# An LSTM recurrence on one core: ScalarE's gates and cell tanh go to PSUM, and the two O sigmoids become one

## The chip, the core and the metric

The kernel runs on one core of a Trainium2 chip. Its time is the device time of one execution in microseconds. Five engines work on it: TensorE (PE; its weight loads are the profile's PEld), VectorE (DVE), ScalarE (ACT), GpSimd (POOL), and SyncE (SP), which issues DMAs. They have queues of their own and meet only at semaphores. There are two on-chip memories: SBUF, and PSUM, in which matmuls leave their results, in 8 banks.

## The reference

The input `x` has 2 sequences of 1024 steps with 256 features. First a modulated projection is added to it, and then the outputs of an LSTM with 256 hidden values, whose start state is `cond_1024`:

```python
x = x + _L0_cond_ref(x, cond_1024, L0_cond_weight)
x = x + _L1_cond_ref(x, cond_1024, L1_cond_Wx, L1_cond_Wh, L1_cond_b)
...
xW = jnp.einsum('ntd,dk->tnk', x, Wx) + b
def step(carry, xw_t):
    prev_h, prev_c = carry
    a = xw_t + prev_h @ Wh
    i = jax.nn.sigmoid(a[:, :Hdim])
    f = jax.nn.sigmoid(a[:, Hdim:2 * Hdim])
    o = jax.nn.sigmoid(a[:, 2 * Hdim:3 * Hdim])
    g = jnp.tanh(a[:, 3 * Hdim:])
    next_c = f * prev_c + i * g
    next_h = o * jnp.tanh(next_c)
```

The 1024 steps depend on each other: `h` of one step is an operand of the next one's product with `Wh`.

## The kernel before, in words

**Before the loop** (about the first 90 us) the kernel transposes `x` so that features lie on the partitions, computes the projection and `xW` with large matmuls, and prepares `Wh` as two 16-bit parts, `wh_p`.

**The layout of a step.** The 256 hidden values are two chunks of 128 partitions (K = 2), and there are B = 2 sequences, so that a gate of a step has only CB = 4 columns. `h` too is kept in two 16-bit parts, `h_parts`; each gate chunk is the sum of products of both parts. All the operations on VectorE and ScalarE have 2 to 12 elements in each partition.

**The matmuls of a step** (`iteration` in the tensor block, L430 to L464; all are recorded at L302, the helper `mm`). First come 12 input matmuls, which put this step's `xW` into PSUM through an identity matrix (`ring`, `ident_b`): for the gates F, G and I seven of them, which wait for `c_done` (the new cell of the step before), and for O the last five, which wait for `o_act` (the sigmoids of O of the step before). Then come 44 matmuls with `h_parts`: 8 for the high part of I (wait `h_hi`), 8 for F (wait `h_lo`, signal `f_mm`), 8 for G (`g_mm`), 8 for the low part of I (`ig_in`), 4 for the first chunk of O (`o0_mm`), 8 for the second chunk of O (`o_mm`).

**The cell** is computed by VectorE and ScalarE in turns:

- L608 DVE sums the two parts of F; L692 ACT takes its sigmoid to `sig_f`; L612 DVE multiplies it by the old cell, into `scan_b`.
- L610 DVE sums G; L695 ACT takes the sigmoid of I and G together (G is computed as 2 sigmoid(2a) - 1, its weights being doubled), into `scan_in`.
- L614 DVE sums the first chunk of O; L697 and L699 ACT take the sigmoids of O's two chunks, into `scan_h`.
- L617 DVE, a scan over 12 elements (4 columns of 3), computes the new cell, reading two SBUF operands and writing PSUM (`c_done`); L701 ACT takes its tanh, into `scan_h` (`t_done`).
- L620 DVE multiplies sigmoid(O) and tanh into the high part of `h` (`h_hi`); L623, another scan, computes the low part (`h_lo`); L627 keeps `h` for the output.

GpSimd prepares the ring of inputs and adds `h` to `xt` in groups of four steps.

**The output** leaves in 8 blocks of 128 steps. In the first iteration of each later block, at four of its eight steps, PE transposes a 128 x 128 tile of the block before into `turned` (L464), and ScalarE copies it out (L707, signal `y_read`). Such a transpose happens 7 x 4 = 28 times. `turned` lies in the bank of G's sum, G_SUM; the transpose waits for `cell_in`, which says that ScalarE has read that bank, and PE waits for the copy (L452) behind the F products of the next step, ahead of its G products.

**What sets the order.** The order is the written order of each engine's block; there is no planner. The loops are L466 to L471: the first block of steps, and for each later block its iteration with transposes and then an inner loop without.

Of the kernel before, what the change touches and what calls it, by code (L numbers as in the profile page):

```python
# [27 lines left out]
P = 128  # L28
# [11 lines left out]
I_BANK, G_SUM, F_BANK, O_BANK, G_BANK, FO_SUM, CELL, O_REST = range(8)  # L40
# [3 lines left out]
def cond_resid_lstm(nc, x, cond, w, wx, wh, bias, out):  # L44
# [11 lines left out]
    with ExitStack() as ctx:  # L56
# [3 lines left out]
        def sem(name):  # L60
            return ctx.enter_context(nc.semaphore(name))
# [40 lines left out]
        scan_in = sb("scan_in", [P, 6 * CB + 2 + 2])  # L102
        scan_a = scan_in[:, 0:3 * CB].rearrange("p (c s) -> p c s", s=3)
        scan_b = scan_in[:, 3 * CB + 2:6 * CB + 2].rearrange("p (c s) -> p c s", s=3)
        sig_ig = scan_in[:, 2:6 * CB + 2].rearrange("p (h c s) -> p h c s", h=2, s=3)[:, :, :, 0]
# [10 lines left out]
        pre_f = banks[FO_SUM][:, 0:CB]  # L116
        pre_o = banks[FO_SUM][:, CB:CB + B]
        pre_g = banks[G_SUM][:, 0:CB]
        pre_ig = psum[:, I_BANK:G_SUM + 1, 0:CB]
        turned = banks[G_SUM][:, BANK - P:BANK]  # L120
# [25 lines left out]
        f_act, o0_act, o_act = sem("f_act"), sem("o0_act"), sem("o_act")  # L146
        cell_in, c_done, t_done = sem("cell_in"), sem("c_done"), sem("t_done")
# [146 lines left out]
        def _(pe):  # L294
# [135 lines left out]
            def iteration(i, n=None):  # L430

                t = i * UNROLL
                for u in range(UNROLL):
                    part = u - TILE_STEP
                    if u % HALF == 0:
                        pe.wait_ge(ring_full, 2 * i + u // HALF + 1)
                    pe.wait_ge(c_done, t + u + 1)
                    input_apart(GATE_F, u, 0, K)
                    input_apart(GATE_G, u, 0, K)
                    input_together(GATE_I, I_BANK, u, 0, K)  # L440
                    pe.wait_ge(o_act, t + u + 1)
                    input_apart(GATE_O, u, 0, 1)
                    last = input_together(GATE_O, O_REST, u, 1, K)
                    if u % HALF == HALF - 1:
                        last.then_inc(ring_used, 1)
                    pe.wait_ge(h_hi, t + u + 1)
                    products(GATE_I, I_BANK, 0, 0, K)
                    pe.wait_ge(h_lo, t + u + 1)
                    products_apart(GATE_F, 0, K).then_inc(f_mm, 1)
                    if n is not None and 0 < part <= B * K:  # L450

                        pe.wait_ge(y_read, n * (B * K) + (part - B * K))  # L452
                    products_apart(GATE_G, 0, K).then_inc(g_mm, 1)
                    products(GATE_I, I_BANK, 1, 0, K).then_inc(ig_in, 1)
                    products_apart(GATE_O, 0, 1).then_inc(o0_mm, 1)
                    products(GATE_O, O_REST, 0, 1, K)
                    products(GATE_O, O_REST, 1, 1, K).then_inc(o_mm, 1)
                    if n is not None and 0 <= part < B * K:

                        b, k = divmod(part, K)  # L460
                        if part == 0:
                            pe.wait_ge(y_whole, n)
                        pe.wait_ge(cell_in, (t + u + 1) * 2)
                        nc.tensor.transpose(turned, y_tile[:, k * B + b, :], ident[:, :]).then_inc(y_turned, 1)  # L464
# [16 lines left out]
        def _(dve):  # L481
# [80 lines left out]
            link(nc.vector.memset(scan_in[:, :], 0.0))  # L562
            nc.vector.memset(scan_a[:, :, 1], 2.0)
            nc.vector.memset(scan_b[:, :, 1], -1.0)
# [20 lines left out]
            nc.vector.memset(pre_f, 0.0).then_inc(h_lo, 1)  # L585
            nc.vector.memset(cell, 0.0).then_inc(c_done, 1)
# [15 lines left out]
            with dve.Fori(0, T // UNROLL) as i:  # L602
                t = i * UNROLL
                for u in range(UNROLL):
# [7 lines left out]
                    nc.vector.tensor_tensor(scan_b[:, :, 2], sig_f[:, :], cell[:, :, 2], ALU.mult).then_inc(cell_in, 1)  # L612
                    dve.wait_ge(o0_mm, step)
                    nc.vector.tensor_reduce(by_chunk(pre_o), parts_of(GATE_O, 1), AX.X, ALU.add).then_inc(o0_sum, 1)  # L614

                    dve.wait_ge(cell_in, both)
                    nc.vector.tensor_tensor_scan(flat(cell), flat(scan_a), flat(scan_b),  # L617
# [3 lines left out]
                                                   in1=scan_h[:, :, 2], op0=ALU.mult, op1=ALU.mult).then_inc(h_hi, 1)  # L621
                    dve.wait_ge(h_hi, step)
                    nc.vector.tensor_tensor_scan(flat(h_parts[:, 1, :, :]), flat(scan_h[:, :, :]), flat(h_parts[:, 0, :, :]),  # L623
# [12 lines left out]
        def _(act):  # L636
# [43 lines left out]
            act.sem_inc(t_done, 1)  # L680

            act.sem_inc(s_out, 16)

            def iteration(i, n=None):

                t = i * UNROLL
                for u in range(UNROLL):
# [59 lines left out]
```

## Times and profile before

| | |
|---|---|
| time, median of 3 runs | 2111.53 us (2111.23 to 2111.78) |
| span of the profiled execution, first to last instruction | 2109.4 us |
| median less span | 2.1 us |
| PE busy | 1884.8 us, 89% |
| PEld busy | 1744.9 us, 83% |
| DVE busy | 1250.0 us, 59% |
| ACT busy | 707.7 us, 34% |
| POOL busy | 480.7 us, 23% |

The span is what the profiled execution's own time was between its first and last instruction; the times of the runs contain 2.1 us more. Busy shares count an instruction from its start to its end; instructions of one engine overlap, and in a serial chain an engine with a low share can still be on the path. A timeline row has the start in us, the duration in us, the engine, the line, the operation and its tiles, and in brackets how long the engine was idle before it and who released it.

### The profile page before, as it was taken

How to read it: one execution, taken by the hardware profiler on the slowest of the kernel's cores; microseconds unless marked ns; L12 is line 12 of the kernel's file. 1: busy time of each engine (PE TensorE's matmuls, PEld its weight loads, DVE VectorE, ACT ScalarE, POOL GpSimd, SP SyncE). 2: the span in 40 equal slices, each digit the busy share in tenths (PEclk: the TensorE clock that was granted, in tenths of full speed). 3: DMA queues.
4: the chain of work that ended last, by engine and by line, in shares of the span. 5: the costliest groups of instructions: out<-in, count | busy, mean ns of one | idle time of the engine just before them, and what ended most of it. 6: DMA issues, size and time to landing. Idle time of an engine off the chain costs nothing. (4 is left out here: it accounts for less than half of the span.)

```text
span 2109.4 us, 138886 instructions
## 1 busy us (share of the span) xinstructions
PE 1884.8 (89%) x57612; PEld 1744.9 (83%) x57612; DVE 1250.0 (59%) x8257; ACT 707.7 (34%) x5179; POOL 480.7 (23%) x1298
## 2 busy tenths in 40 slices
PE   8999999999989998899989999899998999989998
PEld 5588888888878888888878888788887888878887
DVE  3366666666656665566656666566665666656665
ACT  2233333333333333333333333333333333333333
POOL 1122222222222222222222222222222222222221
PEclk9855555555555555555555555555555555555555
DMA  2000000000000000000000000000000000000000
GB/s 85 2 0 0 0 0 7 0 0 0 0 8 0 0 0 1 7 0 0 0 1 7 0 0 0 7 1 0 0 0 8 0 0 0 0 8 0 0 0 5
DMA packets 5214, 7.67 MB, mean 4 GB/s; under 512 B 268, under 2 KB 4632, under 8 KB 5144
## 3 DMA queue, kind: packets, MB, share of 16 engines
q1 hardware_dynamic: 4872, 6.30, 0.9%
q8 instruction: 66, 1.08, 0.2%
q10 hardware_dynamic: 272, 0.26, 0.0%
q14 instruction: 4, 0.03, 0.0%
HBM read 4.46 MB, written 2.10 MB: 3 GB/s over the span
## 5 line engine op out<-in xcount | busy, mean ns | idle before, releaser
L302 PE MATMUL psum<-h_parts,wh_p 128*128 128x2 f16 (+1 forms) x45056 | 1370.9, 166 | 12.6 <-issue 12.4
L302 PEld LDWEIGHTS psum<-h_parts,wh_p 128*128 128x128 f16 x45056 | 1286.7, 104 | 28.9 <-issue 12.8
L302 PE MATMUL psum<-ring,ident_b 128*128 128x4 bf16 (+2 forms) x12288 | 492.6, 168 | 202.1 <-DVE psum L617 179.2
L302 PEld LDWEIGHTS psum<-ring,ident_b 128*128 128x128 bf16 x12288 | 409.7, 105 | 286.2 <-DVE psum L617 260.3
L692 ACT ACTIVATE sig_f<-psum 128x4 f32<-128x4 f32 x1024 | 178.0, 174 | 1136.3 <-DVE psum L608 1136.3
L234 POOL CAST ring<-xw 128x64 bf16 (+1 forms) x256 | 121.3, 474 | 1447.2 <-POOLq L272 1413.2
L608 DVE TENSOR_REDUCE psum<-psum 128x4 f32<-128x8 f32 x1024 | 179.2, 175 | 430.9 <-PE psum L302 430.9
L620 DVE SCALAR_TENSOR_TENSOR h_parts<-scan_h 128x4 f16<-128x4 f32 x1024 | 176.5, 172 | 248.4 <-ACT scan_h L701 248.4
L697 ACT ACTIVATE scan_h<-psum 128x2 f32<-128x2 f32 x1024 | 178.2, 174 | 134.3
L610 DVE TENSOR_REDUCE psum<-psum 128x4 f32<-128x8 f32 x1024 | 179.1, 175 | 52.4 <-PE psum L302 13.5
L623 DVE TENSOR_TENSOR_SCAN h_parts<-scan_h,h_parts 128x12 f16<-128x12 f32 x1024 | 187.5, 183 | 35.1
L695 ACT ACTIVATE scan_in<-psum 128x8 f32<-128x8 f32 x1024 | 185.9, 182 | 56.9 <-PE psum L302 13.7
L617 DVE TENSOR_TENSOR_SCAN psum<-scan_in 128x12 f32<-128x12 f32 x1024 | 198.6, 194 | 0.1
L612 DVE TENSOR_TENSOR scan_in<-sig_f,psum 128x4 f32<-128x4 f32 x1024 | 166.0, 162 | 27.2
L701 ACT ACTIVATE scan_h<-psum 128x4 f32<-128x4 f32 x1024 | 181.0, 177 | 0.1
L614 DVE TENSOR_REDUCE psum<-psum 128x2 f32<-128x4 f32 x1024 | 175.1, 171 | 0.5
L699 ACT ACTIVATE scan_h<-psum 128x2 f32<-128x2 f32 x1024 | 172.0, 168 | 0.0
L627 DVE TENSOR_TENSOR hring<-scan_h 128x4 f32<-128x4 f32 x1024 | 154.6, 151 | 0.0
L240 POOL TENSOR_TENSOR ring<-rest,ring 128x64 bf16<-128x64 f32 x256 | 125.2, 489 | 47.6 <-POOLq L228 47.6
L238 POOL CAST ring<-rest 128x64 bf16<-128x64 f32 x256 | 120.7, 471 | 42.9 <-POOLq L228 42.9
L236 POOL TENSOR_TENSOR rest<-xw,ring 128x64 f32<-128x64 bf16 (+1 forms) x256 | 89.4, 349 | 46.3 <-POOLq L228 46.3
L245 POOL TENSOR_TENSOR xt<-xt,hring 128x16 f32 (+1 forms) x256 | 58.3, 228 | 14.8 <-DVE hring L627 14.8
(81 smaller groups left out, 221.8 us busy)
## 6 DMA issues: line engine op xcount, KB each, us to landing
x_rows<-in_x_dram SPq DMA_DIRECT2D x4, 512.0 KB, 8.6
out_dram<-y_rows SPq DMA_DIRECT2D x7, 256.0 KB, 2.1
wh_sb<-in_L_cond_Wh_dram SPq DMA_DIRECT2D x1, 1024.0 KB, 6.0
wx_sb<-in_L_cond_Wx_dram SPq DMA_DIRECT2D x1, 1024.0 KB, 10.9
w_sb<-in_L_cond_weight_dram ACTq DMA_DIRECT2D x1, 256.0 KB, 2.8
out_dram<-y_rows SPq DMA_DIRECT2D x2, 128.0 KB, 1.7
small_rows<-in_cond_dram SPq DMA_DIRECT2D x1, 2.0 KB
small_rows<-in_L_cond_b_dram SPq DMA_DIRECT2D x1, 4.0 KB
```

Of the source, the lines that this page charges most:

```text
L302: return nc.tensor.matmul(out_, lhs, rhs, start=first, stop=last, skip_group_check=True)
L608: nc.vector.tensor_reduce(by_chunk(pre_f), parts_of(GATE_F, K), AX.X, ALU.add).then_inc(f_sum, 1)
L610: nc.vector.tensor_reduce(by_chunk(pre_g), parts_of(GATE_G, K), AX.X, ALU.add).then_inc(ig_in, 1)
L614: nc.vector.tensor_reduce(by_chunk(pre_o), parts_of(GATE_O, 1), AX.X, ALU.add).then_inc(o0_sum, 1)
L617: nc.vector.tensor_tensor_scan(flat(cell), flat(scan_a), flat(scan_b), 0.0, ALU.mult, ALU.add).then_inc(c_done, 1)
L620: nc.vector.scalar_tensor_tensor(out=h_parts[:, 0, :, 2], in0=scan_h[:, :, 1], scalar=2.0 ** H_SCALE, in1=scan_h[:, :, 2], op0=ALU.mult, o ...
L623: nc.vector.tensor_tensor_scan(flat(h_parts[:, 1, :, :]), flat(scan_h[:, :, :]), flat(h_parts[:, 0, :, :]), 0.0, ALU.mult, ALU.subtract).t ...
L692: nc.scalar.activation(sig_f[:, :], pre_f, ACT.Sigmoid, scale=unscale).then_inc(f_act, 1)
L695: nc.scalar.activation(sig_ig, pre_ig, ACT.Sigmoid, scale=unscale).then_inc(cell_in, 1)
L697: nc.scalar.activation(scan_h[:, 0:B, 1], pre_o, ACT.Sigmoid, scale=unscale).then_inc(o0_act, 1)
L699: nc.scalar.activation(scan_h[:, B:CB, 1], banks[O_REST][:, B:CB], ACT.Sigmoid, scale=unscale).then_inc(o_act, 1)
L701: nc.scalar.activation(scan_h[:, :, 2], cell[:, :, 2], ACT.Tanh).then_inc(t_done, 1)
```

## The change

Four things are edited.

1. The sigmoids of I and G no longer go to SBUF (`scan_in`) but to PSUM (`gates`, in the bank G_SUM), and the cell scan reads them there. `scan_in` is now one operand of 12 elements in SBUF, with f times the old cell and the constants; the other operand is `gates`.
2. The tanh of the cell is computed twice: first to PSUM (`tanh_c`, signal `t_done`), where the product for the high part of `h` reads it, and then to SBUF (`scan_h`, signal `t_kept`), for the scan of the low part, which now waits for `t_kept` as well, and for the row of outputs.
3. The two sigmoids of O become one, which waits for `o0_sum` and `o_mm` and reads two neighbouring banks; for that the banks are put in another order, and the second chunk of O lies at the start of its bank.
4. `turned` moves from the bank G_SUM to O_BANK, in which the parts of O's first chunk are. The transpose now waits for `o0_sum`, VectorE's read of that bank, and not for `cell_in`; and PE's wait for `y_read` moves from ahead of the G products to ahead of the O input matmuls, since these write O_BANK.

```diff
-I_BANK, G_SUM, F_BANK, O_BANK, G_BANK, FO_SUM, CELL, O_REST = range(8)
+G_SUM, I_BANK, F_BANK, O_BANK, G_BANK, CELL, FO_SUM, O_REST = range(8)
...
-        scan_in = sb("scan_in", [P, 6 * CB + 2 + 2])
-        scan_a = scan_in[:, 0:3 * CB].rearrange("p (c s) -> p c s", s=3)
-        scan_b = scan_in[:, 3 * CB + 2:6 * CB + 2].rearrange("p (c s) -> p c s", s=3)
-        sig_ig = scan_in[:, 2:6 * CB + 2].rearrange("p (h c s) -> p h c s", h=2, s=3)[:, :, :, 0]
+        scan_in = sb("scan_in", [P, CB, 3])
...
+        pre_o0 = banks[FO_SUM][:, 0:B]
+        pre_o = psum[:, FO_SUM:O_REST + 1, 0:B]
         pre_g = banks[G_SUM][:, 0:CB]
-        pre_ig = psum[:, I_BANK:G_SUM + 1, 0:CB]
-        turned = banks[G_SUM][:, BANK - P:BANK]
+        pre_ig = psum[:, G_SUM:I_BANK + 1, 0:CB]
+        turned = banks[O_BANK][:, BANK - P:BANK]
+        gates = banks[G_SUM][:, 2 * CB:5 * CB].rearrange("p (c s) -> p c s", s=3)
+        sig_ig = gates[:, :, 1:3].rearrange("p c h -> p h c")
+        tanh_c = banks[G_SUM][:, 6 * CB:7 * CB]
...
                     pe.wait_ge(o_act, t + u + 1)
+                    if n is not None and 0 < part <= B * K:
+                        pe.wait_ge(y_read, n * (B * K) + (part - B * K))
                     input_apart(GATE_O, u, 0, 1)
...
                     products_apart(GATE_F, 0, K).then_inc(f_mm, 1)
-                    if n is not None and 0 < part <= B * K:
-                        pe.wait_ge(y_read, n * (B * K) + (part - B * K))
                     products_apart(GATE_G, 0, K).then_inc(g_mm, 1)
...
-                        pe.wait_ge(cell_in, (t + u + 1) * 2)
+                        pe.wait_ge(o0_sum, t + u + 2)
                         nc.tensor.transpose(turned, y_tile[:, k * B + b, :], ident[:, :]).then_inc(y_turned, 1)
...
-                    nc.vector.tensor_tensor(scan_b[:, :, 2], sig_f[:, :], cell[:, :, 2], ALU.mult).then_inc(cell_in, 1)
+                    nc.vector.tensor_tensor(scan_in[:, :, 2], sig_f[:, :], cell[:, :, 2], ALU.mult).then_inc(cell_in, 1)
...
-                    nc.vector.tensor_tensor_scan(flat(cell), flat(scan_a), flat(scan_b),
+                    nc.vector.tensor_tensor_scan(flat(cell), flat(gates), flat(scan_in[:, :, :]),
                                                  0.0, ALU.mult, ALU.add).then_inc(c_done, 1)
                     dve.wait_ge(t_done, step)
                     nc.vector.scalar_tensor_tensor(out=h_parts[:, 0, :, 2], in0=scan_h[:, :, 1], scalar=2.0 ** H_SCALE,
-                                                   in1=scan_h[:, :, 2], op0=ALU.mult, op1=ALU.mult).then_inc(h_hi, 1)
+                                                   in1=tanh_c, op0=ALU.mult, op1=ALU.mult).then_inc(h_hi, 1)
                     dve.wait_ge(h_hi, step)
+                    dve.wait_ge(t_kept, step)
...
                     act.wait_ge(o0_sum, step)
-                    nc.scalar.activation(scan_h[:, 0:B, 1], pre_o, ACT.Sigmoid, scale=unscale).then_inc(o0_act, 1)
                     act.wait_ge(o_mm, step)
-                    nc.scalar.activation(scan_h[:, B:CB, 1], banks[O_REST][:, B:CB], ACT.Sigmoid, scale=unscale).then_inc(o_act, 1)
+                    nc.scalar.activation(scan_h[:, :, 1].rearrange("p (h b) -> p h b", b=B), pre_o, ACT.Sigmoid, scale=unscale).then_inc(o_act, 1)
                     act.wait_ge(c_done, step)
-                    nc.scalar.activation(scan_h[:, :, 2], cell[:, :, 2], ACT.Tanh).then_inc(t_done, 1)
+                    nc.scalar.activation(tanh_c, cell[:, :, 2], ACT.Tanh).then_inc(t_done, 1)
+                    nc.scalar.activation(scan_h[:, :, 2], cell[:, :, 2], ACT.Tanh).then_inc(t_kept, 1)
```

ScalarE's queue of one step, before (the tiles are output<-input, then the output's shape):

```order
L692 ACTIVATE sig_f<-psum 128x4 [waits f_sum]
L694 REGISTER_ALU
L695 ACTIVATE scan_in<-psum 128x8 [waits ig_in]
L697 ACTIVATE scan_h<-psum 128x2 [waits o0_sum]
L699 ACTIVATE scan_h<-psum 128x2 [waits o_mm]
L701 ACTIVATE scan_h<-psum 128x4 [waits c_done]
```

ScalarE's queue of one step, after:

```order
L698 ACTIVATE sig_f<-psum 128x4 [waits f_sum]
L700 REGISTER_ALU
L701 ACTIVATE psum<-psum 128x2x4 [waits ig_in]
L704 ACTIVATE scan_h<-psum 128x4 [waits o_mm,o0_sum]
L706 ACTIVATE psum<-psum 128x4 [waits c_done]
L707 ACTIVATE scan_h<-psum 128x4
```

There are five activations in a step as before: one sigmoid of O less, one tanh more. The I/G sigmoid and the first tanh write PSUM.

PE's queue in the step behind a transpose, from the last input matmuls of I (`ring`) to the G products (`h_parts`), before:

```order
L302 MATMUL psum<-ring,ident_b 128x4 x3
L302 MATMUL psum<-ring,ident_b 128x4 [waits o_act]
L302 MATMUL psum<-ring,ident_b 128x2 x4
L302 MATMUL psum<-h_parts,wh_p 128x2 [waits h_hi]
L302 MATMUL psum<-h_parts,wh_p 128x2 x7
L302 MATMUL psum<-h_parts,wh_p 128x4 [waits h_lo]
L302 MATMUL psum<-h_parts,wh_p 128x4 x7
L452 ISA
L302 MATMUL psum<-h_parts,wh_p 128x4 [waits y_read]
```

The same piece of PE's queue, after:

```order
L305 MATMUL psum<-ring,ident_b 128x4 x3
L448 ISA [waits o_act]
L305 MATMUL psum<-ring,ident_b 128x4 [waits y_read]
L305 MATMUL psum<-ring,ident_b 128x2 x4
L305 MATMUL psum<-h_parts,wh_p 128x2 [waits h_hi]
L305 MATMUL psum<-h_parts,wh_p 128x2 x7
L305 MATMUL psum<-h_parts,wh_p 128x4 [waits h_lo]
L305 MATMUL psum<-h_parts,wh_p 128x4 x15
```

The wait for ScalarE's copy of the transposed tile stood behind 16 `h_parts` matmuls of the next step; now it stands ahead of all 44 of them and of the five input matmuls of O.

## Rows read from the trace of the kernel before

**Rows 1.** Head of the profile's page.

```profile
span 2109.4 us, 138886 instructions
```

**Rows 2.** Waits of the whole run: engine, line, releaser, us in total, times, longest.

```profile
DVE h_parts L620 <- ACT scan_h L701: 248.4, 1024, 0.2
```

**Rows 3.** Timeline of one ordinary step: start us, duration us, engine, line, operation.

```profile
1002.01 1.34 PE L302 MATMUL psum<-h_parts,wh_p 128*128 128x2 f16 x44
...
1002.64 0.17 DVE L608 TENSOR_REDUCE psum<-psum 128x4 f32<-128x8 f32 x1 [0.38 <-PE psum L302]
...
1002.85 0.17 DVE L610 TENSOR_REDUCE psum<-psum 128x4 f32<-128x8 f32 x1
...
1003.06 0.18 ACT L695 ACTIVATE scan_in<-psum 128x8 f32<-128x8 f32 x1
1003.17 0.17 DVE L614 TENSOR_REDUCE psum<-psum 128x2 f32<-128x4 f32 x1
1003.28 0.19 DVE L617 TENSOR_TENSOR_SCAN psum<-scan_in 128x12 f32<-128x12 f32 x1
1003.38 0.17 ACT L697 ACTIVATE scan_h<-psum 128x2 f32<-128x2 f32 x1
1003.45 0.17 ACT L699 ACTIVATE scan_h<-psum 128x2 f32<-128x2 f32 x1
1003.50 0.18 ACT L701 ACTIVATE scan_h<-psum 128x4 f32<-128x4 f32 x1
...
1003.53 0.48 PE L302 MATMUL psum<-ring,ident_b 128*128 128x8 bf16 x12 [0.18 <-DVE psum L617]
1003.71 0.17 DVE L620 SCALAR_TENSOR_TENSOR h_parts<-scan_h 128x4 f16<-128x4 f32 x1 [0.24 <-ACT scan_h L701]
1003.92 0.18 DVE L623 TENSOR_TENSOR_SCAN h_parts<-scan_h,h_parts 128x12 f16<-128x12 f32 x1
...
1003.94 1.34 PE L302 MATMUL psum<-h_parts,wh_p 128*128 128x2 f16 x44
```

**Rows 4.** Setup, by shape: count, busy us, mean ns; ScalarE reading SBUF.

```profile
L658 ACT ACTIVATE root<-var 128x4 f32<-128x4 f32 x1 | 0.2, 205 | 5.9 <-DVE var L512 5.9
...
L655 ACT ACTIVATE sig_f<-scales 128x1 f32<-128x1 f32 x1 | 0.2, 186 | 0.0
```

**Rows 5.** The page's groups of small operations: busy us, mean ns.

```profile
L701 ACT ACTIVATE scan_h<-psum 128x4 f32<-128x4 f32 x1024 | 181.0, 177 | 0.1
...
L627 DVE TENSOR_TENSOR hring<-scan_h 128x4 f32<-128x4 f32 x1024 | 154.6, 151 | 0.0
...
L623 DVE TENSOR_TENSOR_SCAN h_parts<-scan_h,h_parts 128x12 f16<-128x12 f32 x1024 | 187.5, 183 | 35.1
```

**Rows 6.** Single lines L612 and L617: duration ns min/median/max.

```profile
L612 DVE TENSOR_TENSOR scan_in<-sig_f,psum x1024: 153/163/164, 92.2 to 2104.1; 128x4 f32<-128x4 f32 x171
...
L617 DVE TENSOR_TENSOR_SCAN psum<-scan_in x1024: 191/192/280, 92.4 to 2104.3; 128x12 f32<-128x12 f32 x171
```

**Rows 7.** Timeline of VectorE where G's sum came late.

```profile
593.15 0.17 DVE L610 TENSOR_REDUCE psum<-psum 128x4 f32<-128x8 f32 x1 [2.39 <-PE psum L302]
593.24 0.15 DVE L612 TENSOR_TENSOR scan_in<-sig_f,psum 128x4 f32<-128x4 f32 x1
```

**Rows 8.** Timeline of a step with a transpose and its copy.

```profile
343.47 0.17 DVE L608 TENSOR_REDUCE psum<-psum 128x4 f32<-128x8 f32 x1 [0.41 <-PE psum L302]
...
343.90 0.18 ACT L695 ACTIVATE scan_in<-psum 128x8 f32<-128x8 f32 x1
344.01 0.17 DVE L614 TENSOR_REDUCE psum<-psum 128x2 f32<-128x4 f32 x1
...
344.13 0.48 PE L464 MATMUL psum<-ident,y_tile 128*128 128x128 f32 x1
...
344.64 0.27 ACT L707 COPY y_rows<-psum 128x128 f32<-128x128 f32 x1
...
344.77 1.33 PE L302 MATMUL psum<-h_parts,wh_p 128*128 128x2 f16 x44
```

More of the change, by code:

```diff
@@ L114, in cond_resid_lstm @@
         banks = [psum[:, i, :] for i in range(8)]
-        pre_f = banks[FO_SUM][:, 0:CB]
-        pre_o = banks[FO_SUM][:, CB:CB + B]
+        pre_f = banks[FO_SUM][:, CB:2 * CB]
+        pre_o0 = banks[FO_SUM][:, 0:B]
+        pre_o = psum[:, FO_SUM:O_REST + 1, 0:B]
         pre_g = banks[G_SUM][:, 0:CB]
-        pre_ig = psum[:, I_BANK:G_SUM + 1, 0:CB]
-        turned = banks[G_SUM][:, BANK - P:BANK]
+        pre_ig = psum[:, G_SUM:I_BANK + 1, 0:CB]
[3 more added lines that the diff above has]
+        tanh_c = banks[G_SUM][:, 6 * CB:7 * CB]
         cell = banks[CELL][:, 0:3 * CB].rearrange("p (c s) -> p c s", s=3)
@@ L145, in cond_resid_lstm @@
         ig_in = sem("ig_in")
-        f_act, o0_act, o_act = sem("f_act"), sem("o0_act"), sem("o_act")
-        cell_in, c_done, t_done = sem("cell_in"), sem("c_done"), sem("t_done")
+        f_act, o_act = sem("f_act"), sem("o_act")
+        cell_in, c_done, t_done, t_kept = sem("cell_in"), sem("c_done"), sem("t_done"), sem("t_kept")
         y_whole, y_turned, y_read = sem("y_whole"), sem("y_turned"), sem("y_read")
@@ L388, in together @@
             def together(bank, first, last):
+                first, last = (first - 1, last - 1) if bank == O_REST else (first, last)
                 return banks[bank][:, B * first:B * last].rearrange("p (c b) -> p c b", b=B)
@@ L560, in _ @@
                 add_projection(n)
-            link(nc.vector.memset(scan_in[:, :], 0.0))
-            nc.vector.memset(scan_a[:, :, 1], 2.0)
-            nc.vector.memset(scan_b[:, :, 1], -1.0)
+            nc.vector.memset(scan_in[:, :, 0], 2.0)
+            nc.vector.memset(scan_in[:, :, 1], -1.0)
             link(nc.vector.memset(scan_h[:, :, :], 0.0))
@@ L585, in _ @@
             nc.vector.memset(pre_f, 0.0).then_inc(h_lo, 1)
+            link(nc.vector.memset(gates, 0.0))
             nc.vector.memset(cell, 0.0).then_inc(c_done, 1)
@@ L611, in _ @@
                     dve.wait_ge(f_act, step)
-                    nc.vector.tensor_tensor(scan_b[:, :, 2], sig_f[:, :], cell[:, :, 2], ALU.mult).then_inc(cell_in, 1)
+                    nc.vector.tensor_tensor(scan_in[:, :, 2], sig_f[:, :], cell[:, :, 2], ALU.mult).then_inc(cell_in, 1)
                     dve.wait_ge(o0_mm, step)
-                    nc.vector.tensor_reduce(by_chunk(pre_o), parts_of(GATE_O, 1), AX.X, ALU.add).then_inc(o0_sum, 1)
+                    nc.vector.tensor_reduce(by_chunk(pre_o0), parts_of(GATE_O, 1), AX.X, ALU.add).then_inc(o0_sum, 1)
                     dve.wait_ge(cell_in, both)
-                    nc.vector.tensor_tensor_scan(flat(cell), flat(scan_a), flat(scan_b),
+                    nc.vector.tensor_tensor_scan(flat(cell), flat(gates), flat(scan_in[:, :, :]),
                                                  0.0, ALU.mult, ALU.add).then_inc(c_done, 1)
@@ L680, in _ @@
             act.sem_inc(t_done, 1)
+            act.sem_inc(t_kept, 1)
             act.sem_inc(s_out, 16)
```

## The prediction

> **What bounds the kernel now.** The first view to read is the timeline of one step, since 1024 steps of a serial recurrence fill nearly the whole span [rows 1]. From the first `h_parts` matmul of one step to that of the next it is 1.93 us [rows 3], and in that time the engines hand over to each other: PE's matmuls, then VectorE, ScalarE, VectorE, ScalarE, VectorE, and PE again. The list of waits says the same for the tail of the step: L620 waits for the tanh L701 in all 1024 steps [rows 2]. So PE's 89% is no bound by itself, and what counts is which of two operands comes last at each hand-over. I read them off [rows 3]:
>
> - L608 (1002.64) and L610 (1002.85) start 0.21 apart: eight matmuls, 0.026 each. Eight more (low part of I) put the start of L695 at 1003.06, where it is; L610's own end, 1003.02, with 0.04 of hand-over says 1003.06 too. Four more (O's first chunk) put L614 at 1003.17, where it is. So up to L695 and L614 PE sets the time, and the change does nothing there.
> - L617 (1003.28) starts 0.04 behind L695's end and 0.11 behind L614's start. Then one chain is left: L617, L701, L620, then PE's `h_parts` matmuls (high part), and L623 hangs on L620.
> - PE's 12 input matmuls start at 1003.53, behind L617, and at 0.026 to 0.028 each are issued by about 1003.86; the `h_parts` matmuls start at 1003.94. PE has some 0.08 us of slack there, which follows L617.
>
> **The change part by part, for an ordinary step.** Call what ScalarE saves by writing PSUM instead of SBUF w. No row of before shows ScalarE writing PSUM. The nearest rows show what SBUF costs it at the other end: reading SBUF and writing SBUF, a tanh took 186 ns (1 element) and a square root 205 ns (4 elements) [rows 4], while the loop's tanh from PSUM takes 177 ns [rows 5]. That is 9 to 28 ns, and I take w = 19, the middle. For the ends: VectorE's scan is slower into PSUM than into SBUF, 192 against 183 ns for 12 elements [rows 5, 6], so that w could be -9; and +28 at the top.
>
> The Trainium skill ("ScalarE: Activation LUTs", section "Step-by-step: what each stage is for") says that PSUM is the lower-latency destination of an ACTIVATE, without a number for the destination; its table in "VectorE: DVE Perf Modes" (the section on the TRN2 errata) has 172 cycles from PSUM against 224 from SBUF, 43 ns at its 1.2 GHz, as an estimate. Were w 43, the sum below would give some 24 us less. This trace has the sign at the source end, with 9 to 28 ns.
>
> 1. I/G sigmoid to PSUM, on the chain. It ends w earlier. But L617 also stands behind L614 on VectorE. There L617 is 0.11 behind [rows 3]; the closest that an instruction followed such a reduction is 0.09 (L610 to L612, when the latter's operand had long been there) [rows 7]. So at most 0.02 can be had, both figures being rounded to 0.01: I take 15 ns, with 0 and 20 as ends.
> 2. The scan reads one operand from PSUM. L612, with one operand in PSUM, took 153 ns at the least, which is when it doesn't wait [rows 6, 7]; L627, the same operation with both in SBUF and unwaiting, 151 ns [rows 5]. So +2 ns. Upper end +11, from L612's median 163 against L627's 151; lower end 0.
> 3. First tanh to PSUM, on the chain: -w = -19, not capped, since PE's slack of 80 ns is larger, and ScalarE is free: the one O sigmoid has its operands at 1003.38 (o_mm: eight matmuls after L614's; o0_sum: L614's end and 0.04), while the tanh starts at 1003.50; L699 followed L697 after 0.07 [rows 3].
> 4. L620 reads one operand from PSUM: +2, as in 2.
> 5. The second tanh starts some 0.07 behind the first and ends by about 1003.75; with the hand-over, its reader L623 could go at 1003.79 and today goes at 1003.92, behind L620 [rows 3]. It costs nothing. If that cover were gone, every ns beyond 0.13 would count.
> 6. One O sigmoid instead of two: not on the chain; its end (1003.56) comes before that of L699 today (1003.62), so PE's wait for `o_act` isn't late either. Nothing.
>
> Sum: -15 + 2 - 19 + 2 = -30 ns in a step.
>
> **The 28 steps behind a transpose.** Today the transpose costs nothing: the `h_parts` matmuls start at 344.77, 1.30 behind L608 (343.47) [rows 8], as in an ordinary step (1003.94 - 1002.64) [rows 3]. After the change:
>
> - The transpose waits for L614 to end, not L695. L614 starts at 0.54 (counted from L608) and ends at 0.71; the transpose started 0.05 behind L695's end (343.90 + 0.18, then 344.13). So it starts at 0.76.
> - The copy today starts 0.51 behind the transpose (344.64 - 344.13). So at 1.27; it takes 0.27: 1.54.
> - PE resumes 0.05 later, 1.59, and has five input matmuls of O yet to do, 5 x 0.028 = 0.14. The `h_parts` matmuls start at 1.73, not 1.30.
>
> Today the wait for this copy (ends at 344.91) stands ahead of the G products, the seventeenth matmul from 344.77 on, 345.20: covered. The new place has no cover, and everything after it in the step waits. Cost: 28 x 0.43 = 12.0 us; and these steps don't get the 30 ns.
>
> **Sum.** (1024 - 28) x 0.030 = 29.9 us less, 12.0 us more: -17.9 us. Against the profiled span of 2109.4 that is 2091.5; with the 2.1 us by which the median of 2111.53 lies above the span, 2093.6 us. I say 2094.
>
> What measurement can tell from no change is 0.2%, 4.2 us: 2107.3 to 2115.8.
>
> **Rivals.**
>
> *The copy's wait outweighs the gain (slower).* Mechanism: the moved `y_read` wait as above, with w near 0. It decides below a gain of 8 ns a step: 996 x 0.008 = 8.0 less, 12.0 more, 4 us slower. With w = 0 and the two PSUM reads at +2 each, the step is 4 ns longer: 4 + 12 = +16, so 2127.5. With w = -9 it is 22 longer, +34: 2145. For it: no row shows such a write, and VectorE writes PSUM more slowly. Against it: ScalarE handles PSUM faster at the source end. 18%.
>
> *VectorE has no room, or pays for PSUM (same).* If L617 can't come closer to L614 than today, only the tanh counts: -19 + 4 = -15 ns, -14.9 + 12.0 = -2.9: 2108.6. The same results nearly if both PSUM reads cost 11 ns: -15 - 19 + 22 = -12 ns, -12.0 + 12.0 = 0: 2111.5. For it: 0.11 is near 0.09, and both are rounded. Against: L617 starts just when L695's result can be there, and 153 is near 151 ns. 16%. The Trainium skill ("VectorE: DVE Perf Modes", the errata table) gives VectorE 120 cycles from PSUM and 58 from SBUF, an estimated 65 ns for each of two reads; that would add 2 x 65 ns to each of 996 steps, 129 us. The rows, with 2 ns between L612 and L627, don't bear it out, and I give that size 2% of the slower 18.
>
> *More than forecast.* With w = 28 and the full 20 ns: -20 - 28 + 4 = -44, -43.8 + 12.0 = -31.8: 2079.7. The same, 2081.6, if the copy's wait is somehow covered. 20%.
>
> The forecast itself, 2083 to 2105, has 46%. So faster by over 0.2% is 66%, within 0.2% 16%, slower 18%. The range of 8 in 10 goes from 2074 (w a little above its upper end) to 2120 (w near 0).
>
> Not counted: stalls of PE's queue when the loop passes from block to block, which the order leaves alone; and some L617 of up to 280 ns [rows 6], 2 ns in the mean, which may go or stay when one of its operands is in PSUM.
>
> **What would show it.** Right: L701's successor to PSUM at 158 ns or so and the I/G sigmoid at 163; the scan at 194; an ordinary step of 1.90 us; 28 steps of about 2.36 us in which the copy releases PE. Wrong in step 1: the scan still 0.11 behind the reduction of O and over 0.04 behind the sigmoid. Wrong in 2 or 4: the scan or the product over 200 or 180 ns. Wrong in 5: L623's successor waiting for the second tanh. The prediction fails as a whole if ScalarE's times into PSUM are no shorter than into SBUF.

## The result, and the profile of the changed kernel

The change made the kernel slower, by 0.8%: 2128.36 us (median of 4 runs, 2127.03 to 2129.67) against 2111.66 (2111.23 to 2112.52), a ratio of 1.0079 with a 95% interval of 1.0065 to 1.0093. The forecast of 2094 and its range of 2074 to 2120 were wrong.

The page of the changed kernel, span and groups (busy us, mean ns, then idle time before and what ended it). New names of lines: L612 is F's sum (before L608), L618 the sum of O's first chunk (L614), L621 the scan (L617), L624 and L628 the products of h (L620, L623), L701 the I/G sigmoid (L695), L704 the one O sigmoid (L697, L699), L706 the tanh (L701), L707 the second tanh.

```profile
span 2125.2 us, 140921 instructions
...
L624 DVE SCALAR_TENSOR_TENSOR h_parts<-scan_h,psum 128x4 f16<-128x4 f32 x1024 | 169.7, 166 | 269.1 <-ACT psum L706 269.1
...
L704 ACT ACTIVATE scan_h<-psum 128x4 f32<-128x4 f32 x1024 | 179.2, 175 | 229.2 <-PE psum L305 229.0
L707 ACT ACTIVATE scan_h<-psum 128x4 f32<-128x4 f32 x1024 | 210.2, 205 | 0.0
L621 DVE TENSOR_TENSOR_SCAN psum<-psum,scan_in 128x12 f32<-128x12 f32 x1024 | 195.4, 191 | 0.0
...
L701 ACT ACTIVATE psum<-psum 128x8 f32<-128x8 f32 x1024 | 165.9, 162 | 56.8 <-PE psum L305 10.4
L706 ACT ACTIVATE psum<-psum 128x4 f32<-128x4 f32 x1024 | 173.8, 170 | 0.2 <-issue 0.2
```

The I/G sigmoid came down from 182 to 162 ns, as forecast. The tanh only went from 177 [rows 5] to 170. The timeline of one ordinary step of the changed kernel:

```profile
1002.26 0.17 DVE L612 TENSOR_REDUCE psum<-psum 128x4 f32<-128x8 f32 x1 [0.38 <-PE psum L305]
...
1002.68 0.16 ACT L701 ACTIVATE psum<-psum 128x8 f32<-128x8 f32 x1
1002.79 0.17 DVE L618 TENSOR_REDUCE psum<-psum 128x2 f32<-128x4 f32 x1
1002.90 0.19 DVE L621 TENSOR_TENSOR_SCAN psum<-psum,scan_in 128x12 f32<-128x12 f32 x1
1003.07 0.17 ACT L704 ACTIVATE scan_h<-psum 128x4 f32<-128x4 f32 x1 [0.22 <-PE psum L305]
...
1003.14 0.17 ACT L706 ACTIVATE psum<-psum 128x4 f32<-128x4 f32 x1
...
1003.19 0.21 ACT L707 ACTIVATE scan_h<-psum 128x4 f32<-128x4 f32 x1
1003.34 0.17 DVE L624 SCALAR_TENSOR_TENSOR h_parts<-scan_h,psum 128x4 f16<-128x4 f32 x1 [0.26 <-ACT psum L706]
```

Counted from the start of F's sum, the O sigmoid starts at 0.81 (1003.07 - 1002.26), where the prediction gave it operands at 1003.38 - 1002.64 = 0.74 [rows 3]. The tanh starts 0.07 behind that, at 0.88; before it started at 0.86 [rows 3]. Numbers with three figures after the point are means over the steps of the whole timeline. An ordinary step is one that is neither behind a transpose nor over 2.2 us. After the change 105 of the 983 ordinary steps are longer than the rest, and have a column of their own:

| from the start of F's sum, us | before | after, 878 steps | after, the other 105 |
|---|---|---|---|
| scan starts | 0.639 | 0.636 | 0.635 |
| first (or only) O sigmoid starts | 0.738 | 0.811 | 0.811 |
| last O sigmoid ends | 0.975 | 0.986 | 0.986 |
| tanh starts / ends | 0.866 / 1.043 | 0.881 / 1.052 | 0.941 / 1.099 |
| high product starts | 1.075 | 1.085 | 1.132 |
| ordinary step | 1.934 | 1.933 | 1.98 |

Over all 983 the ordinary step is 1.939. So most steps are as long as before, where 30 ns less was forecast: the tanh ends 9 ns later, and the high product, which is 6 ns shorter (166 against 172), makes up for most of that.

The span grew by 15.8 us. All but the 28 steps behind a transpose went from 1957.4 to 1961.0 us, +3.6 (29.9 less was forecast); those 28 went from 54.5 to 66.3 us, +11.8 (12.0 was forecast). So of the 15.8 us three quarters are the copy's wait, which was forecast; what was not is that nothing came in to pay for it. The 105 long steps last 1.98 to 1.99 (one lasts 2.19). They are always the second of the eight steps of an iteration of the inner loop of blocks 1 to 7 (7 x 15 = 105). In them the tanh starts 0.13 behind the O sigmoid, and takes 158 ns; 5.4 us in all. This is one, in ScalarE's timeline:

```profile
1010.80 0.17 ACT L704 ACTIVATE scan_h<-psum 128x4 f32<-128x4 f32 x1 [0.22 <-PE psum L305]
1010.93 0.16 ACT L706 ACTIVATE psum<-psum 128x4 f32<-128x4 f32 x1
1011.00 0.17 ACT L707 ACTIVATE scan_h<-psum 128x4 f32<-128x4 f32 x1
```

A step behind a transpose, changed kernel: the copy now stands in the chain.

```profile
343.66 0.17 DVE L612 TENSOR_REDUCE psum<-psum 128x4 f32<-128x8 f32 x1 [0.40 <-PE psum L305]
...
344.19 0.17 DVE L618 TENSOR_REDUCE psum<-psum 128x2 f32<-128x4 f32 x1
...
344.42 0.48 PE L468 MATMUL psum<-ident,y_tile 128*128 128x128 f32 x1
...
344.93 0.27 ACT L713 COPY y_rows<-psum 128x128 f32<-128x128 f32 x1
...
345.25 0.29 PE L305 MATMUL psum<-ring,ident_b 128*128 128x4 bf16 x5 [0.19 <-ACT y_rows L713]
...
345.41 1.31 PE L305 MATMUL psum<-h_parts,wh_p 128*128 128x2 f16 x44
```

Transpose at 0.76, copy at 1.27, five matmuls, and the `h_parts` matmuls at 1.75 against 1.30 before [rows 8]. The prediction had 0.76, 1.27 and 1.73.

### The profile page after: what moved, and what is told of

Read it like the earlier page. It is cut to its first block and busy times, and to the rows that moved or that the text cites. A ratio compares the mean times of both kernels' runs of the same rounds, so it can differ in the third digit from the quotient of the medians.

```text
span 2125.2 us, 140921 instructions
## 1 busy us (share of the span) xinstructions
PE 1900.1 (89%) x57612; PEld 1741.5 (82%) x57612; DVE 1238.3 (58%) x8257; ACT 719.3 (34%) x5179; POOL 480.2 (23%) x1298
## 5 line engine op out<-in xcount | busy, mean ns | idle before, releaser
L612 DVE TENSOR_REDUCE psum<-psum 128x4 f32<-128x8 f32 x1024 | 178.8, 175 | 439.0 <-PE psum L305 439.0
L624 DVE SCALAR_TENSOR_TENSOR h_parts<-scan_h,psum 128x4 f16<-128x4 f32 x1024 | 169.7, 166 | 269.1 <-ACT psum L706 269.1
L704 ACT ACTIVATE scan_h<-psum 128x4 f32<-128x4 f32 x1024 | 179.2, 175 | 229.2 <-PE psum L305 229.0
L707 ACT ACTIVATE scan_h<-psum 128x4 f32<-128x4 f32 x1024 | 210.2, 205 | 0.0
L614 DVE TENSOR_REDUCE psum<-psum 128x4 f32<-128x8 f32 x1024 | 179.2, 175 | 51.8 <-PE psum L305 12.2
L628 DVE TENSOR_TENSOR_SCAN h_parts<-scan_h,h_parts 128x12 f16<-128x12 f32 x1024 | 187.5, 183 | 34.8
L621 DVE TENSOR_TENSOR_SCAN psum<-psum,scan_in 128x12 f32<-128x12 f32 x1024 | 195.4, 191 | 0.0
L701 ACT ACTIVATE psum<-psum 128x8 f32<-128x8 f32 x1024 | 165.9, 162 | 56.8 <-PE psum L305 10.4
L618 DVE TENSOR_REDUCE psum<-psum 128x2 f32<-128x4 f32 x1024 | 174.7, 171 | 0.5
L706 ACT ACTIVATE psum<-psum 128x4 f32<-128x4 f32 x1024 | 173.8, 170 | 0.2 <-issue 0.2
## 6 DMA issues: line engine op xcount, KB each, us to landing
wx_sb<-in_L_cond_Wx_dram SPq DMA_DIRECT2D x1, 1024.0 KB, 10.5
```

The costliest lines, as they stand in the source:

```text
L612: nc.vector.tensor_reduce(by_chunk(pre_f), parts_of(GATE_F, K), AX.X, ALU.add).then_inc(f_sum, 1)
L614: nc.vector.tensor_reduce(by_chunk(pre_g), parts_of(GATE_G, K), AX.X, ALU.add).then_inc(ig_in, 1)
L618: nc.vector.tensor_reduce(by_chunk(pre_o0), parts_of(GATE_O, 1), AX.X, ALU.add).then_inc(o0_sum, 1)
L621: nc.vector.tensor_tensor_scan(flat(cell), flat(gates), flat(scan_in[:, :, :]), 0.0, ALU.mult, ALU.add).then_inc(c_done, 1)
L624: nc.vector.scalar_tensor_tensor(out=h_parts[:, 0, :, 2], in0=scan_h[:, :, 1], scalar=2.0 ** H_SCALE, in1=tanh_c, op0=ALU.mult, op1=ALU.mu ...
L701: nc.scalar.activation(sig_ig, pre_ig, ACT.Sigmoid, scale=unscale).then_inc(cell_in, 1)
```

## The experiments

Medians are in us; ratios are against the kernel before, on the same chip. The kernel before's own median was 2109.52 to 2111.66 from one series of experiments to the next, so a difference between versions of different series is good to about 2 us. Code is cut down to what differs.

**The two O sigmoids apart again.** Everything else as in the changed kernel.

```
-act.wait_ge(o0_sum, step); act.wait_ge(o_mm, step)
-activation(scan_h[:, :, 1], pre_o)
+act.wait_ge(o0_sum, step); activation(scan_h[:, 0:B, 1], pre_o0).then_inc(o0_act)
+act.wait_ge(o_mm, step);   activation(scan_h[:, B:CB, 1], banks[O_REST][:, 0:B])
```

> The changed kernel with the two sigmoids of O restored (the first waits for o0_sum, the second for o_mm); all else as changed. Theory A (the merged sigmoid of O starts at 0.81 us behind L612, because o_mm comes only then, and the tanh must keep 0.07 us behind it on ScalarE): the tanh starts at about 0.866 instead of 0.881, an ordinary step is 0.015 us shorter, and the time falls by about 15 us to 2113; if the 105 slow steps (0.05 us each) belong to that order of ScalarE's queue too, by 5 more. Rival B (the tanh is late because its operand, the cell, or the second tanh holds it): no change, 2128.

2114.88, ratio 1.0021 (1.0011 to 1.0031): 13.5 less than the changed kernel, of which 12.1 show in its steps. No step of 1.98 is left, and an ordinary one lasts 1.927. So the merging costs 12 ns a step, 5 of them by the 105 long steps. But the step stays far above 1.90, and the tanh has its 182 ns although it goes to PSUM. Its timeline shows it tied to the sigmoid ahead:

```profile
1001.82 0.17 DVE L612 TENSOR_REDUCE psum<-psum 128x4 f32<-128x8 f32 x1 [0.41 <-PE psum L305]
...
1002.55 0.17 ACT L703 ACTIVATE scan_h<-psum 128x2 f32<-128x2 f32 x1 [0.15 <-DVE psum L618]
1002.62 0.17 ACT L705 ACTIVATE scan_h<-psum 128x2 f32<-128x2 f32 x1
1002.68 0.18 ACT L707 ACTIVATE psum<-psum 128x4 f32<-128x4 f32 x1
```

**No second tanh.** The changed kernel less `activation(scan_h[:, :, 2], ...).then_inc(t_kept, 1)` and VectorE's wait for it.

> The changed kernel without the second tanh: scan_h's tanh is never written, so the low part of h and the kept h are computed from old data; durations don't depend on data. Theory A: the second tanh is off the chain; the first starts at 0.881 as before, the ordinary step stays, time 2126 to 2128. If the slow second step of each loop iteration is ScalarE running out of issued instructions, it may move or go: 5 us less. Rival B (the second tanh lengthens the first, 170 instead of 158 ns, or delays the scan of the low part): 12 ns less in each step, 2116.

2121.52, ratio 1.0055 (1.0038 to 1.0071), 6.8 less. The first tanh starts as late as with the second behind it (0.880), so it is not this one that holds it; what goes are the steps of 1.98 (5.4 us). Here the low part of `h` comes from old data.

**The transpose's wait put back under cover.** In the steps with a copy, the wait for `y_read` and O's input matmuls of its first chunk stand ahead of O's products instead of ahead of the `h_parts` matmuls.

```
+late = n is not None and 0 < part <= B * K
-if late: pe.wait_ge(y_read, ...)
-input_apart(GATE_O, u, 0, 1)
+if not late: input_apart(GATE_O, u, 0, 1)
 ...
 products(GATE_I, I_BANK, 1, 0, K).then_inc(ig_in, 1)
+if late: pe.wait_ge(y_read, ...); input_apart(GATE_O, u, 0, 1)
```

> The changed kernel, but in the 28 steps behind a transpose the two input matmuls that write O_BANK stand behind the low-part products of I, and the wait for the copy (y_read) stands ahead of them there. If the moved wait costs the 0.42 us in these steps that the trace shows (2.37 instead of 1.95): those steps become about 1.99 (two matmuls of 0.027 on the path), and the time falls by about 10.5 us to 2118. Rival (the transpose itself, waiting for o0_sum, holds PE): hardly less than 2128.

2116.51, ratio 1.0029 (1.0018 to 1.004): 11.8 less. The steps behind a transpose come down from 2.37 to 1.99, 10.7 us in all 28. The `h_parts` matmuls now start while the copy runs:

```profile
346.75 0.27 ACT L717 COPY y_rows<-psum 128x128 f32<-128x128 f32 x1
346.82 0.99 PE L305 MATMUL psum<-h_parts,wh_p 128*128 128x2 f16 x32
...
347.67 0.19 PE L305 MATMUL psum<-ring,ident_b 128*128 128x4 bf16 x2
```

**One matmul more behind O's last.** Is a PE with nothing more to do late to signal its last matmul? Behind `o_mm` PE does one more matmul into an unused part of F's bank, with a wait for `f_sum` ahead of it, which has long been met by then.

> The changed kernel with one more matmul, of constants into unused columns of F's bank, behind the last O product that signals o_mm. Eight matmuls of 0.027 behind o0_mm's hand-over (0.533) would put o_mm at 0.75 behind L612, but the sigmoid of O starts at 0.81. Theory C (the last matmul of a burst signals late when nothing follows it): the sigmoid starts at about 0.76, the tanh at 0.863, and the time falls by about 17 us to 2111. Rival D (0.81 has another cause: the path to ScalarE or two waits on one instruction): no change, 2128.

2130.52, ratio 1.0093 (1.0076 to 1.0109); the sigmoid starts at 0.810 as before. That theory fell.

**Only one sigmoid of O, with only one wait.** The split version less the sigmoid of O's first chunk, which then comes from old data.

> The changed kernel with O's sigmoids apart, and the first of them left out (O's first chunk then comes from old data). The second then has nothing just ahead of it on ScalarE. Theory E (o_mm's own arrival sets it: 0.81 us behind L612, as the merged sigmoid starts there with an idle engine too): the sigmoid starts at 0.81, the tanh about 0.06 behind it, and ends no sooner than 0.067 behind the sigmoid's end, 1.04; the ordinary step stays at 1.93, the time at about 2115. Rival F (0.805 is the distance to the first sigmoid, and the merged one is late by its two waits or two banks): the sigmoid starts at about 0.76 and ends at 0.93, the tanh into PSUM takes 158 ns instead of 182, the ordinary step is 0.02 us shorter, and the time is about 2095.

2089.55, ratio 0.9903 (0.9886 to 0.9919). The sigmoid starts at 0.746, the tanh is tied to nothing and takes 158 ns, and the ordinary step lasts 1.901:

```profile
L705 ACT ACTIVATE psum<-psum 128x4 f32<-128x4 f32 x1024 | 161.8, 158 | 0.0
```

So with the O sigmoid out of the way the forecast's step is there. The sigmoid that waits for PE's last matmul of O starts at 0.746 here, with one wait, and at 0.811 in the changed kernel, with two.

**Split O and late transpose wait together.**

> The changed kernel with O's sigmoids apart and the two input matmuls of O's first chunk and the copy's wait behind I's low products in the 28 steps: both repairs together. If they add: ordinary steps of 1.927 and steps behind a transpose of 1.98: 2114.9 less 10.6 is 2104, 0.3% faster than before. If they don't (each repair shortens the same wait): about 2112.

2104.41, ratio 0.9975 (0.9965 to 0.9984): 10.5 below the split version alone, so the two parts add up.

**No sum of O's first chunk.** The split version less L618 (left out) and its waits; ScalarE waits for PE's matmuls instead.

> The changed kernel with O's sigmoids apart and without VectorE's sum of O's first chunk (L618); the first sigmoid of O reads an old value as soon as o0_mm is there. Theory G (the cell scan starts 0.103 behind L618 because two operations on VectorE can't follow closer, which takes most of the 20 ns by which the I/G sigmoid now ends earlier): the scan starts at 0.62 behind L612, 0.03 behind the I/G sigmoid's end. But the tanh, if its end is tied to O's sigmoid, still ends at 1.04: the step stays at 1.927 and the time at about 2113. Rival (the scan waits for something else, such as its f product): it starts at 0.636 as before.

2067.47, ratio 0.9801 (0.9785 to 0.9818), step 1.885. The scan starts 0.619 from F's sum instead of 0.636: this sum is what holds the scan, whose start the sigmoid's 20 ns therefore moved by only 3. The time fell much further than the 2113 expected. Without the sum the first O sigmoid starts at 0.533 instead of 0.737, so the second starts at 0.745 instead of 0.805, and the tanh is tied to nothing and takes 158 ns. The transpose's wait for the sum is left out too, and the steps behind a transpose take 2.16. So 2067 is not what the sum alone is worth.

```profile
1002.62 0.17 DVE L611 TENSOR_REDUCE psum<-psum 128x4 f32<-128x8 f32 x1 [0.41 <-PE psum L305]
...
1003.04 0.16 ACT L698 ACTIVATE psum<-psum 128x8 f32<-128x8 f32 x1
...
1003.24 0.19 DVE L618 TENSOR_TENSOR_SCAN psum<-psum,scan_in 128x12 f32<-128x12 f32 x1
```

**The merging alone, on the kernel before.** Both sigmoids of O as one with two waits; sigmoid and tanh of the cell to SBUF as before, no second tanh.

> The kernel before with nothing but the merged sigmoid of O (and the banks reordered for it); gates and tanh go to SBUF, the transposes stay in G's bank. If the merge costs by itself: the tanh starts 0.07 behind the sigmoid's 0.81, at 0.88 instead of 0.866, takes 177 ns, and the ordinary step is 0.012 to 0.015 us longer, 12 to 15 us more than before, 2124, with or without 5 us of slow steps. If the merge costs nothing by itself: 2111.

2120.33, ratio 1.0049 (1.0032 to 1.0066). So this edit alone costs some 10 us, with no PSUM destination and no second tanh.

**One O sigmoid behind one semaphore.** All of the changed kernel's work is done here, but VectorE's sum and PE's last O product count up the same semaphore, by two in a step:

```
-act.wait_ge(o0_sum, step); act.wait_ge(o_mm, step)
+act.wait_ge(o_in, both)
```

with `.then_inc(o_in, 1)` at both sources, and PE's wait ahead of the transpose on `o_in` too.

> The changed kernel, but VectorE's sum of O's first chunk and PE's last O product signal one semaphore, o_in, and the merged sigmoid waits once, for 2 per step. Theory H (the second wait on one instruction is what puts the merged sigmoid at 0.81 instead of 0.746, where a sigmoid with one wait started when nothing was ahead of it): it starts at 0.75, the tanh at 0.86 and takes 158 ns, the ordinary step is about 1.901, the slow steps of the second step in a loop iteration may go or stay, and the time is about 2090. Rival I (reading two banks in one instruction makes it late): 0.81 still, 2128.

2090.42, ratio 0.9912 (0.9895 to 0.9929): 38 us less than the changed kernel, for one wait instead of two. The sigmoid reads the same banks and does the same as there:

```profile
span 2087.5 us, 139916 instructions
...
1001.90 0.17 DVE L611 TENSOR_REDUCE psum<-psum 128x4 f32<-128x8 f32 x1 [0.40 <-PE psum L305]
...
1002.64 0.17 ACT L702 ACTIVATE scan_h<-psum 128x4 f32<-128x4 f32 x1 [0.16 <-PE psum L305]
1002.76 0.16 ACT L704 ACTIVATE psum<-psum 128x4 f32<-128x4 f32 x1
```

It starts at 0.745 in the mean, with ScalarE idle for 0.16 ahead of it instead of 0.22, the step lasts 1.901, no step of 1.98 is left. The rival, that reading two banks delays it, fell.

**The half sigmoid of O with two waits.** The version with only one sigmoid, plus `act.wait_ge(o0_sum, step)` ahead of its wait.

> As t1_one_o (O's first sigmoid left out, the second one alone, reading one bank), but it waits for o0_sum and o_mm, two semaphores. O's first chunk comes from old data. Theory H: it starts at 0.81 instead of 0.746, and the time goes from 2089.5 to about 2110 to 2120. Rival I (two banks): it stays at 0.746, 2089.5.

2127.66, ratio 1.0088 (1.0071 to 1.0105), the sigmoid at 0.811 again. Between this and its twin one wait differs, and 38 us. The added wait is met no later than the other: `o0_sum` at 0.738, `o_mm` at 0.745, by the starts of the sigmoids that wait for one of them alone.

**One semaphore and late transpose wait.** The best version.

> u1_one_wait with the repair of s3_late_o (O_BANK's two input matmuls and the copy's wait behind I's low products in the 28 steps). If the two add: 2090 less 10.6, 2080, 1.5% faster than before. If theory H is wrong: 2117.

2079.11, ratio 0.9858 (0.9841 to 0.9874): faster than before by 1.4%, and against the changed kernel 0.978 (0.9858 / 1.0079; 0.975 to 0.981 by the ends of both intervals). Its page:

```profile
span 2077.1 us, 139909 instructions
...
L627 DVE SCALAR_TENSOR_TENSOR h_parts<-scan_h,psum 128x4 f16<-128x4 f32 x1024 | 168.6, 165 | 229.5 <-ACT psum L708 229.5
...
L706 ACT ACTIVATE scan_h<-psum 128x4 f32<-128x4 f32 x1024 | 180.2, 176 | 163.3 <-PE psum L305 163.1
...
L708 ACT ACTIVATE psum<-psum 128x4 f32<-128x4 f32 x1024 | 161.8, 158 | 0.0
```

**The same with one tanh, to SBUF.** What is the tanh's PSUM destination worth? (The I/G sigmoid stays in PSUM; there is no second tanh.)

> u3_one_wait_late_o with one tanh, to SBUF, read there by VectorE; the I/G sigmoid stays in PSUM. If the tanh to PSUM is worth its 158 against 176 ns, and VectorE's product 165 against 171 ns, once O's sigmoid is early: the step is 0.024 us longer, 2104. If O's sigmoid still ties the tanh's end: no difference from u3_one_wait_late_o.

2102.55, ratio 0.9967 (0.9954 to 0.9979): 23.4 more than with it. The tanh takes 176 ns against 158, and the product, which now reads it from SBUF, 171 against 165.

**The best version with the gates in SBUF.** `gates = sb("gates", [P, CB, 3])` in place of the PSUM tile.

> u3_one_wait_late_o with the I/G sigmoid and the cell scan's operand in SBUF again, the tanh in PSUM. The scan starts 0.103 behind VectorE's sum of O's first chunk in u3_one_wait_late_o, and would start 0.034 behind the end of the I/G sigmoid, 0.640, if that goes to SBUF (182 ns): 3 to 4 ns a step, 2083. If the gates in PSUM are worth their full 20 ns: 2099.

2088.97, ratio 0.9897 (0.9881 to 0.9914): 9.9 more. The ordinary step is 1.911 against 1.901, some 10 ns more, where 3 to 4 were expected from the scan's start, or 20 from the sigmoid's duration. The scan starts 3 ns later (0.640 against 0.637); the rest is mostly in its own duration, mean 196 ns against 190. The view of its line has min/median/max in ns, here and then in the best version:

```profile
L624 DVE TENSOR_TENSOR_SCAN psum<-gates,scan_in x1024: 190/192/336, 92.9 to 2082.8; 128x12 f32<-128x12 f32 x171
```

```profile
L624 DVE TENSOR_TENSOR_SCAN psum<-psum,scan_in x1024: 190/190/191, 92.9 to 2072.1; 128x12 f32<-128x12 f32 x171
```

**A second wait that is met beforehand.** The one-semaphore version, plus `act.wait_ge(f_sum, step)`, which counts F's sum (ended at 0.17) and so is met some 0.5 us earlier, written ahead of the wait for `o_in`.

> u1_one_wait with a second wait on the merged sigmoid of O, for f_sum, which has been met since 0.17 us behind L612's start. If any second wait on an instruction of ScalarE costs: the sigmoid starts at 0.81, 2116 to 2128. If only a wait that is met late costs: it starts at 0.745 and the time stays at 2090.

2126.16, ratio 1.0079 (1.0062 to 1.0095). The sigmoid is at 0.81 again:

```profile
span 2123.4 us, 140940 instructions
...
1002.22 0.17 DVE L611 TENSOR_REDUCE psum<-psum 128x4 f32<-128x8 f32 x1 [0.41 <-PE psum L305]
...
1003.03 0.18 ACT L703 ACTIVATE scan_h<-psum 128x4 f32<-128x4 f32 x1 [0.22 <-PE psum L305]
```

The instruction count rose by 1024: the second wait is an instruction of its own in ScalarE's queue. The trace records it, as an EVENT_SEMAPHORE at L702, the line of the wait written last. In this step:

```profile
L702 ACTq EVENT_SEMAPHORE  x1: 17/17/17, 1003.0 to 1003.0; - x1
```

It waits for `o_in`; it runs 0.743 into the step (median), and the sigmoid starts 0.067 behind it.

**These two waits swapped.** `o_in` first, then `f_sum`; nothing else differs.

> w1_met_wait with its two waits written in the other order (first o_in, then f_sum). Theory J (the wait written last is carried by an instruction of its own ahead of the sigmoid, and the sigmoid is handed to the engine only when that is through; here that is f_sum, met long before, as t_kept is on VectorE): the sigmoid starts at 0.745, the time is 2090. Theory K (any second wait on a ScalarE instruction costs 0.065): 0.81, 2126.

2090.09, ratio 0.9906 (0.9889 to 0.9922), with as many instructions:

```profile
span 2087.4 us, 140940 instructions
...
1002.05 0.17 DVE L611 TENSOR_REDUCE psum<-psum 128x4 f32<-128x8 f32 x1 [0.41 <-PE psum L305]
...
1002.80 0.17 ACT L703 ACTIVATE scan_h<-psum 128x4 f32<-128x4 f32 x1 [0.16 <-PE psum L305]
```

The sigmoid is at 0.745. The instruction of its own is still there, but now it waits for `f_sum`, and runs 0.43 into the step (median), long before `o_in` is met. In this step:

```profile
L702 ACTq EVENT_SEMAPHORE  x1: 17/17/17, 1002.5 to 1002.5; - x1
```

So it is neither the number of waits nor that of instructions, and theory J holds. The wait written last is carried by an instruction of its own, and the operation starts no sooner than 0.067 behind that one. When the wait written last is the one met last, the operation starts 0.065 later than when it is written first.

**The changed kernel with its two waits swapped.** `o_mm` first, `o0_sum` last.

> The changed kernel with nothing but the two waits of the merged sigmoid in the other order (first o_mm, then o0_sum). Theory J: the instruction of its own now waits for o0_sum, met at 0.738, and the sigmoid follows 0.065 behind it, at 0.80 instead of 0.81; the time falls by 5 to 10 us to about 2120, no more, since both operands come late. Theory K: no change, 2128.

2124.32, ratio 1.0064 (1.0047 to 1.0081), the sigmoid at 0.804, and the steps of 1.98 stay. The sigmoid starts where theory J puts it: the wait written last is for VectorE's sum, met at 0.738, and 0.065 behind that is 0.803. The time is 4 us below the changed kernel's, less than the 5 to 10 expected, and the two intervals overlap. Both waits of this sigmoid are met late, so swapping hardly helps it; one semaphore does.

**The merging on the kernel before, with one semaphore.**

> t4_merge_only (the kernel before with the merged sigmoid of O) with one semaphore for O's two operands; gates and tanh in SBUF. The sigmoid starts at 0.746 instead of 0.812, the tanh at 0.867 when the cell is there, and takes 176 ns: the ordinary step is 1.934 as before, 2110, so that the merge by itself neither gains nor costs. If the sigmoid's end had been what tied the tanh of the kernel before: faster than before by up to 10.

2105.19, ratio 0.9975 (0.9965 to 0.9985): from 10 us slower with two waits to 5 us faster with one. The second branch of the expectation came true: the tanh ends at 1.041 instead of 1.043, the product takes 170 ns instead of 172, and the ordinary step is 1.929.

## Why the prediction was wrong

**The step that failed is 6, "One O sigmoid instead of two: not on the chain", and with it step 3's "ScalarE is free".** The operands of the O sigmoid do come at 0.74, as step 3 had it, but with two waits it starts at 0.81 and ends at 0.98 to 0.99. The tanh then starts 0.07 behind its start and ends 0.066 to 0.068 behind its end: 0.986 and 1.052 in the changed kernel, 0.974 and 1.041 in the split one (there it starts only 0.054 behind, and takes 182 ns). The untied tanh of the one-semaphore version has 0.920 and 1.018. So the tanh couldn't end before about 1.05, whatever it wrote to; its 18 ns (176 to 158) went into its waiting for the sigmoid. The two steps fail in two parts. With the sigmoids apart the ordinary step came down by 7 ns instead of 30, which is step 3's share; merging them under two waits put 12 ns back on, which is step 6's. The kernel before stood at this edge already (0.975 and 1.043), as its rows could have told: L699 starts 0.07 behind L697 and the tanh close behind L699 [rows 3]. The prediction read the slack of the O sigmoid from the time of its operands, and asked if its end was early enough for PE, but not whether it was for the next activation, nor what a second wait costs.

- *Step 1, 15 ns: wrong in its way, right in its bound.* The sigmoid is 20 ns shorter, but the scan comes no closer than 0.103 to the start of O's sum; its start moved by 3 ns. The prediction named this (scan still 0.11 behind the reduction). In the best version the gates in PSUM are nevertheless worth 10 ns a step, most of it in the scan's duration, for which the prediction left 2 ns open.
- *Steps 2 and 4, +2 ns each: wrong in sign.* Both operations became shorter: the scan 191 against 194 ns in the mean, the product 166 against 172 (it waited for the tanh in both kernels). The Trainium skill ("VectorE: DVE Perf Modes", the TRN2 errata table) would have had an estimated 65 ns more for each, and the measurement decides against it here.
- *Step 3, w = 19: right.* 18 ns for the tanh and 20 for the sigmoid. The experiment that sends the tanh back to SBUF is 23.4 us slower; 6 of the 24 ns behind that are the product's.
- *Step 5: right in most steps.* Without the second tanh the ordinary step is 1.933 as with it; but with a late O sigmoid the 105 steps of 1.98 come only with it.
- *The 28 steps, +12.0 us: right*, +11.8, and gone with the wait put back.
- *The rivals.* The slower one gave 2127.5 and the time was 2128.36: that is luck, since it wanted w near 0, and w was 18 to 20. Its part on the copy holds. "VectorE has no room" holds for the scan's start. A rival in which ScalarE's own queue holds the tanh was missing.

Without the late O sigmoid the forecast's total is there: the one-semaphore version has a step of 1.901 against 1.934, 33 ns less where 30 were forecast, and 2090.42 us where 2094 was. That it fits so well is partly luck. The tanh gave its 19 ns, but the scan's start only 3 where 15 were counted, and the scan and the product gave 3 and 7 where 2 more were counted for each.

**Open.** Why a late two-wait sigmoid with two tanhs behind it gives 105 steps of 1.98, always the second of an iteration of the inner loop, isn't settled: they are there in the changed kernel and in each version with a late sigmoid and two tanhs, and in none of the others with two tanhs. Nor is why the scan with both operands in SBUF takes up to 336 ns at times.

## What to carry to other kernels

Before an operation is said to be off the chain, see what follows it on its own engine: an instruction that starts 0.07 or less behind its forerunner is tied to it, and a gain in its duration goes into that tie. Where two producers feed one instruction and both come late, let both count up one semaphore (this is sound only if neither can be a step ahead of the other; here both wait for the `h` that the consumer leads to); where one comes early, write its wait last. When an edit moves a wait ahead of work that used to cover it, price it by the steps in which it is met late (here 28 x 0.42 us), and put it behind that work again.

## What the runs showed of the hardware that was not expected

- The second wait of a ScalarE operation is an instruction of its own in the queue (1024 more for one more wait in 1024 steps). It carries the wait written last, and the operation starts no sooner than 0.067 us behind it: 0.811 against 0.745 if the wait written last is the last met. VectorE's low product, whose last-written wait is met early, starts 0.034 behind the end of the high one: no such delay.
- ScalarE's activations start as close as 0.054 to 0.07 us behind each other, in the mean, while each takes 158 to 205 ns; their ends stayed 0.063 us or more apart (0.061 at the least).
- A ScalarE destination in PSUM takes 18 ns (tanh, 4 elements) or 20 ns (sigmoid, 8 elements) less than one in SBUF; VectorE's small operations didn't take longer with one operand in PSUM (scan 191 against 194 ns, product 165 against 171).
